# Routing two chunks in the expert phase, choosing part 1 inside the last chain, and a PSUM bank for each of the last local tiles

## What is computed

```
a = x + global_latent_attn(rmsnorm(x, norm1_w))      # causal, 16 heads of 8, 4 key/value heads
a = a + local_gqa_attn(rmsnorm(a, norm2_w))          # causal, window of 32 keys
x = layernorm(x + a)
probs = sigmoid(x @ router_w.T + routing_bias)       # 8 experts
topk_p, topk_idx = top_k(probs, 2); topk_p /= sum(topk_p)
shared = (silu(x @ sg_w.T) * (x @ su_w.T)) @ sd_w.T
routed = sum over the 2 experts of topk_p * (silu(x @ wg[e].T) * (x @ wu[e].T)) @ wd[e].T
out = layernorm(x + shared + routed)
```

## Time and profile before

| what | us |
|---|---|
| median of 3 runs | 815.64 |
| lowest and highest | 811.75, 817.01 |
| the profiled execution | 819.62 |
| its span, first to last instruction | 817.9 |
| TensorE busy / VectorE busy | 641.7 / 518.1 |
| ScalarE busy / GpSimd busy | 406.9 / 376.5 |

### The profile page before, as it was taken

One profiled execution on the slowest core, in us unless ns is written; L12 is line 12 of the kernel. 1 busy time (PEld: TensorE's weight loads), 2 busy tenths in 40 slices (PEclk: granted clock), 3 DMA queues, 4 the chain that ended last, 5 costly groups with the idle time before them and its releaser, 6 DMA issues. The chain is left out here.

```text
span 817.9 us, 12163 instructions
## 1 busy us (share of the span) xinstructions
PE 641.7 (78%) x3942; PEld 350.3 (43%) x3942; DVE 518.1 (63%) x1340; ACT 406.9 (50%) x562; POOL 376.5 (46%) x414
## 2 busy tenths in 40 slices
PE   2337888988998887899976697975278999996991
PEld 1203332233453333444333243444266676664881
DVE  2566864456996557898459966475854774332685
ACT  0225766866766775567754454740012544343244
POOL 3397633424544443443322676702324147777511
PEclk9958888999999998999878797996568999999895
DMA  8133555400000000000000001100003123323332
GB/s 253 55 107 104 188 160 186 146 1 1 1 1 1 1 1 14 2 13 14 14 1 0 25 27 37 34 14 0 7 21 93 41 71 91 105 82 114 115 104 65
DMA packets 38126, 47.22 MB, mean 58 GB/s; under 512 B 8961, under 2 KB 35233, under 8 KB 37409
## 3 DMA queue, kind: packets, MB, share of 16 engines
q1 hardware_dynamic: 26976, 35.10, 14.2%
q0 software_dynamic: 4352, 9.05, 3.2%
q10 hardware_dynamic: 6736, 2.30, 1.2%
HBM read 35.29 MB, written 28.98 MB: 79 GB/s over the span
## 5 line engine op out<-in xcount | busy, mean ns | idle before, releaser
L781 ACT ACTIVATE prob<-ps_s 128x1024 f32<-128x1024 f32 x320 | 309.4, 1025 | 197.9 <-PE ps_s L1109 129.0
L1142 PE MATMUL ps_v<-prob,va 128*32 128x512 f32 x1152 | 173.1, 685 | 16.5 <-POOL prob L703 15.8
L1109 PE MATMUL ps_s<-qs,ks 32*128 32x512 f16 x576 | 106.5, 410 | 33.9 <-ACT prob L781 30.5
L916 DVE STREAM_TRANSPOSE sums<-ps_v 128x512 f32<-128x512 f32 x64 | 45.7, 714 | 86.3 <-PE ps_v L1136 44.1
L703 POOL TENSOR_SCALAR_AFFINE_SELECT prob<-prob 128x1024 f32<-128x1024 f32 x64 | 70.4, 1118 | 51.1 <-ACT prob L781 50.7
L1109 PEld LDWEIGHTS ps_s<-qs,ks 32*128 32x128 f16 x576 | 25.2, 92 | 146.7 <-ACT prob L781 97.5
L1349 POOL DMA_INDIRECT y_rows<-y,to_row x72 | 69.5, 966 | 37.0 <-issue 19.8
L1136 PE MATMUL ps_v<-prob,vd 128*128 128x256 f32 (+1 forms) x312 | 72.1, 384 | 17.3 <-DVE marked L936 17.2
L1371 ACT ACTIVATE gated<-ps_gu 128x512 f32<-128x512 f32 x52 | 31.0, 598 | 89.1 <-PE ps_gu L1565 67.4
L1136 PEld LDWEIGHTS ps_v<-prob,vd 128*128 128x128 f32 x312 | 59.3, 215 | 31.4 <-DVE prob L943 15.7
L1565 PE MATMUL ps_gu<-weights,rows_t 128*128 x144 | 68.0, 594 | 0.5 <-ACT rows_t L1376 0.5
(11 more groups left out here) (200 smaller groups left out, 1036.9 us busy)
## 6 DMA issues: line engine op xcount, KB each, us to landing
x_rows<-in_blank SPq DMA_DIRECT2D x8, 2112.0 KB, 9.4
rows<-x_rows SPq DMA_DIRECT2D x72, 66.0 KB, 2.1
chosen_y<-y_rows SPq DMA_DIRECT2D x8, 512.0 KB, 6.8
weights<-in_weights SPq DMA_DIRECT2D x1, 3456.0 KB, 13.6
marked<-in_hidden SPq DMA_DIRECT2D x4, 512.0 KB, 5.1
out<-result ACTq DMA_DIRECT2D x8, 256.0 KB, 2.3
r_in<-in_hidden SPq DMA_DIRECT2D x7, 256.0 KB, 2.8
y_rows<-y,to_row POOLq DMA_INDIRECT x72, 2.4
```

Of the source, the lines that this page charges most:

```text
L781: act.activation(probs_at(n, 0, SLOT_COLS), scores_at(n, 0, SLOT_COLS), ACT.Exp, scale=HD ** -0.5 / GAIN ** 2).then_inc(exped, 1)
L916: dve.transpose(sums[:].rearrange("p r b v -> p (r b v)"), ps_v[bank_of[q]][:].rearrange("p r q -> p (r q)")).then_inc(sums_turned, 1)
L1109: last = pe.matmul(scores_at(n, j * BANK, BANK).rearrange("p (r q) -> p r q", r=REP), ks[b % QUERY_BATCHES][rows, kt * P:(kt + 1) * P], qs ...
L1142: last = pe.matmul(bank[g * VW:(g + 1) * VW, :, :], va[b % VALUE_BATCHES][:, kt, g, :], probs_at(n + g // 2, g % 2 * BANK, BANK).rearrange ...
```

## The change

Chunks 6 and 7 are both routed in the expert phase (`LATE = CHUNKS - 2`), which adds, norms and turns eight tiles there: the statistics on VectorE in steps 1 and 2, the norm itself as eight Identity activations on ScalarE in step 3 (`late_tokens`), the turns at steps 4 and 5, logits of all eight tiles at step 6 and the exponential at step 7. The turn at step 45 goes. Chunk 6 has no chain in the attention phase any more. Part 1 is chosen at steps 326 to 345, and all its 16 scatters are issued at steps 352 to 367. Its blocks are laid in two lists (`LISTS`), rows of chunks 0 to 3 first, and `EARLY_PAIRS` falls to 24. The last part's 16 scatters stand ahead of pair 6. The `combine` of chunks 0 to 3 moves to steps 34, 36, 37 and 38, that of the others up by one. There are four `result` buffers. The last four local tiles have their slots at steps 356 to 359, the last two of them use the side banks `ps_p`, and the projection follows two steps behind the product.

The diff, cut to its core:

```diff
 TURNS = 3
 LOCAL_STEPS = 2
-POST = 3
+LAST_LOCALS = 4
+POST, LAST_POST = 3, 2
 VALUE_BATCHES, QUERY_BATCHES = 3, 3
 SHARES = 3
 FINAL = SHARES - 1
...
 SHARE_ENDS = tuple(2 * tiles - EXPERTS for tiles in TILES_SO_FAR[:-1]) + (POSITIONS,)
 SHARE_BEGINS = (0,) + SHARE_ENDS[:-1]
 SHARE_POSITIONS = tuple(end - begin for begin, end in zip(SHARE_BEGINS, SHARE_ENDS))
-EARLY_POSITIONS = SHARE_BEGINS[FINAL] + 2 * SHARE_TILES[0] + EXPERTS - 1 - SHARE_ENDS[0]
+EARLY_POSITIONS = SHARE_BEGINS[FINAL] + EXPERTS
 CAPACITY = TILES
 X_BLOCKS = EXPERTS * CAPACITY + EXPERTS
-LISTS = tuple(EXPERTS * (2 if part == FINAL else 1) for part in range(SHARES))
-LATE = CHUNKS - 1
-TO_ROW, FIRST_EXPERT, GAIN, WEIGHT = range(D, D + 4)
+LISTS = tuple(EXPERTS * (2 if part else 1) for part in range(SHARES))
+LATE = CHUNKS - 2
+TO_ROW, FIRST_EXPERT, GAIN_AT, WEIGHT = range(D, D + 4)
 ROW = D + 4
 SCAN, ENDS = 8, 8
 SHIFTS = tuple(tuple(2 ** n for n in range(6) if 2 ** n < tiles) for tiles in SHARE_TILES)
...
           (34, "choose", "experts")]
 SENDS_FROM = 29
 SEND = [(SENDS_FROM + i * 3 // 2, "send", i) for i in range(2 * SHARE_TILES[0])]
-SENT_INSIDE = 8
 INSIDE = [CHOOSE + SEND,
-          CHOOSE[:1] + [(34, "choose", "prob"), (34, "choose", "first"), (35, "choose", "second"), (35, "choose", "third"),
-                        (36, "choose", "weights"), (37, "choose_rank"), (38, "choose", "totals"), (38, "choose", "scan"),
-                        (39, "choose", "slots"), (40, "choose", "slot1"), (41, "choose", "slot2")]
-          + [(47 + i, "send", i) for i in range(SENT_INSIDE)]]
-ROUTE_AT = {0: 172, 1: 188, 2: 210, 3: 0, 4: 0, 5: 0, 6: 344}
+          CHOOSE[:1] + [(17, "choose", "prob"), (17, "choose", "first"), (20, "choose", "second"), (20, "choose", "third"),
+                        (26, "choose", "weights"), (28, "choose_rank"), (34, "choose", "totals"), (34, "choose", "scan"),
+                        (35, "choose", "slots"), (35, "choose", "slot1"), (36, "choose", "slot2")]
+          + [(43 + i, "send", i) for i in range(2 * SHARE_TILES[1])]]
+ROUTE_AT = {0: 172, 1: 188, 2: 210, 3: 0, 4: 0, 5: 0}
 P_DVE = [["one_plus", "prob", "top1", "is1", "place1", "first1", "mark", "pick1", "others",
...
-    for i, _ in enumerate(range(B * TPB - sum(len(v) for v in LOCAL_INSIDE.values()))):
-        add_local((j + 1 + i) % 2)
-        step += LOCAL_STEPS
+    left = B * TPB - sum(len(v) for v in LOCAL_INSIDE.values())
+    for i in range(left):
+        add_local(SIDES + i - (left - SIDES) if i >= left - SIDES else (j + 1 + i) % 2)
+        step += 1 if i >= left - LAST_LOCALS else LOCAL_STEPS
...
+        def sums_bank(q):
+
+            return ps_v[bank_of[q]][:] if bank_of[q] < 2 else ps_p[bank_of[q] - 2][:].rearrange("p (r q) -> p r q", r=REP)
+
...
                         pe.wait_ge(rope, rope_value(chunk_number[chunk], 1, "values"))
-                if w == firsts[q] and before[q] is not None:
+                if w == firsts[q] and bank_of[q] >= 2:
+                    take_side(bank_of[q] - 2, added, q + 1)
+                elif w == firsts[q] and before[q] is not None:
                     pe.wait_ge(added, before[q] + 1)
...
 MARKED_AT = {ROUTED_AT[m] + 2: m // GROUP for m in range(0, PAIRS, GROUP)}
 LATE_BEGIN, LATE_AT = 1, 4
 PICK_AT = {1: {"blocks": 4, "ends": 4, "starts": 5, "past": 5, "rows": 6, "experts": 6},
-           2: {"prob": 7, "first": 7, "second": 8, "third": 8, "weights": 8, "totals": 10, "scan": 10, "slots": 11, "slot1": 11,
+           2: {"prob": 8, "first": 8, "second": 9, "third": 9, "weights": 9, "totals": 11, "scan": 11, "slots": 11, "slot1": 12,
                "slot2": 12, "blocks": 13, "ends": 13, "starts": 14, "past": 14, "rows": 15, "experts": 15}}
 TURN_AT = {c: SHARED_AT[c * CT // 2] - 3 if c * CT // 2 in SHARED_LAST else SHARED_FIRST.index(c * CT // 2) // 2 - 1
-           for c in range(LATE)} | {LATE: LATE_AT}
-GATHERED_AT = {0: 37, 1: 38, 2: 39, 3: 40, 6: 47, 4: 48, 7: 49, 5: 50}
+           for c in range(LATE)} | {c: LATE_AT + c - LATE for c in range(LATE, CHUNKS)}
+LOGITS_AT = LATE_AT + 2
+GATHERED_AT = {0: 34, 1: 36, 2: 37, 3: 38, 6: 46, 4: 47, 7: 48, 5: 49}
 LAST = 2
 IN_TIME = [f for f, when in GATHERED_AT.items() if when <= SHARED_AT[2 * f] + LAST]
 END_AT = {f: SHARED_AT[2 * f + 1] + LAST if f in IN_TIME else when + 1 for f, when in GATHERED_AT.items()}
 END_STEPS = 2
 FINALS_AFTER = PAIRS - 1
-BEFORE_SEND = {2: 2}
+FINAL_SENDS = 6
+RESULTS = 4
...
         def _(pool):
             def late_power():
 
                 pool.wait_ge(l_dve, nth(LATE_STEPS, "var_eps"))
-                pool.tensor_tensor(rstd[CHUNKS][:], rstd[CHUNKS][:], st["half"][:], ALU.pow).then_inc(l_rstd, 1)
-
-            def dispatch(part):
-
-                if part == FINAL:
-                    pool.wait_ge(p_dve[part], picked(part, "index2"))
-                    pool.wait_ge(l_dve, nth(LATE_STEPS, f"token{CT - 1}"))
-                for i in range(SENT_INSIDE if part < FINAL else 0, 2 * SHARE_TILES[part]):
-                    t, k = SHARE_FIRST[part] + i // 2, i % 2
-                    pool.indirect_dma_start(
-                        x_rows, bass.IndirectOffsetOnAxis(ap=index[:, t, k:k + 1], axis=0), st["marked"][:, t, :], None
-                    ).then_inc(dispatched[part], 16)
+                pool.tensor_tensor(l_rstd[:], l_rstd[:], st["half"][:], ALU.pow).then_inc(l_powered, 1)
+
+            def dispatch():
+
+                pool.wait_ge(p_dve[FINAL], picked(FINAL, "index2"))
+                pool.wait_ge(l_tokens, LATE_TILES)
+                for t in range(SHARE_FIRST[FINAL], TILES):
+                    for k in range(2):
+                        pool.indirect_dma_start(
+                            x_rows, bass.IndirectOffsetOnAxis(ap=index[:, t, k:k + 1], axis=0), st["marked"][:, t, :], None
+                        ).then_inc(dispatched[FINAL], 16)
 
             def send_y(m):
 
@@ -1352,13 +1363,12 @@
 
             def power(f):
                 pool.wait_ge(f_dve[f], nth(END, "var_eps"))
-                pool.tensor_tensor(rstd[f][:], rstd[f][:], st["half"][:], ALU.pow).then_inc(f_rstd, 1)
-
-            dispatch(1)
+                pool.tensor_tensor(rstd[f][:], rstd[f][:], st["half"][:, 0:CT], ALU.pow).then_inc(f_rstd, 1)
+
             late_power()
             for m in range(PAIRS):
-                if m in BEFORE_SEND:
-                    dispatch(BEFORE_SEND[m])
+                if m == FINAL_SENDS:
+                    dispatch()
                 send_y(m)
...
-                act.dma_start(out.rearrange("b (t p) d -> p (b t) d", p=P)[:, chunk(f), :], result[f % 2][:]
-                              ).then_inc(out_stored[f % 2], 16)
+                place = results.index(f)
+                act.wait_ge(f_result, CT * (place + 1))
+                act.dma_start(out.rearrange("b (t p) d -> p (b t) d", p=P)[:, chunk(f), :], result[place % RESULTS][:]
+                              ).then_inc(out_stored[place % RESULTS], 16)
 
...
+            def late_tokens():
+
+                act.wait_ge(l_dve, nth(LATE_STEPS, "shift"))
+                for t in range(LATE_TILES):
+                    of = x[:, LATE * CT + t, :]
+                    act.activation(of, of, ACT.Identity, bias=l_shift[:, t:t + 1], scale=l_rstd[:, t:t + 1]).then_inc(l_tokens, 1)
 
             for c in turned_at(-1):
                 move_tokens(c)
@@ -1405,9 +1424,11 @@
                         move_rows(SEQUENCE[step + 1][1])
                 if 0 <= step - 1 < len(SEQUENCE) and routed(step - 1):
                     move_hidden(step - 1)
+                if step == LATE_AT - 1:
+                    late_tokens()
                 for c in turned_at(step):
                     move_tokens(c)
-                if step == LATE_AT + 2:
+                if step == LOGITS_AT + 1:
                     act.wait_ge(l_dve, nth(LATE_STEPS, "logit"))
                     act.activation(choice["logits"][FINAL][:], choice["logits"][FINAL][:], ACT.Exp, scale=-1.0).then_inc(p_exped[FINAL], 1)
...
+                if n == LATE_BEGIN + 1:
+                    for t in range(LATE_TILES):
+                        late_step()(f"moments{t}", dve.bn_aggr, l_moments[:, t, :], l_stats[:, t, :])
+                    late_step()("var_eps", dve.tensor_scalar, l_rstd[:], l_moments[:, :, 1], LN_EPS, None, ALU.add)
                 if n == LATE_AT - 1:
-                    dve.wait_ge(l_rstd, 1)
-                    scale(late_step(), "token", x[:, late, :], x[:, late, :], CHUNKS)
-                if n == LATE_AT + 1:
+                    dve.wait_ge(l_powered, 1)
+                    late_step()("shift", dve.scalar_tensor_tensor, l_shift[:], l_moments[:, :, 0], -1.0, l_rstd[:], ALU.mult, ALU.mult)
+                if n == LOGITS_AT:
                     dve.wait_ge(l_logits, 1)
-                    late_step()("logit", dve.tensor_tensor, choice["logits"][FINAL][:, SHARE_TILES[FINAL] - CT:, :],
```

(3 more changed lines are left out.)

102 lines of the change are left out of this document (48 added, 54 removed).

## The result

The changed kernel takes 806.64 us (median of 19 runs, 804.25 to 817.09) against 817.01 us (19 runs, 811.75 to 823.46) for the kernel before, measured beside it: ratio 0.988, 95% interval 0.986 to 0.991. It is faster by some 10 us (1.2 per cent, with 1 outside the interval), half of the 20 forecast, and just above the predicted range.

What follows compares the result with a forecast made beforehand. Routed steps run through TensorE almost alone, with time lost at four places; -11.2 + 6.5 - 10.9 - 4.4 = -20.0 us takes the median from 815.64 to 795.6 us, range 787 to 806.

Steps and rivals of the forecast that it cites:

- Last chain: End of attention phase: `k_rows` at 580.7 instead of 585.98, first scores of the last tiles at 584.0 instead of 591.41.
- Last four tiles: Last local tiles of attention: TensorE ends at 601.7, but GpSimd's 16 scatters close the phase at 604.1; -11.2 us with the chain.
- so E moves to 604.4: Expert phase start, 615.54 before: 16 scatters cost 20.2 us from 583.9, end at 604.1 and set the start; -11.2 us.
- E: The start of the expert phase, set 0.27 us behind the last work before it; 615.54 before, 604.4 forecast.
- a start 0.27 us behind the last work before it: End of attention phase: margin assumed between the last work there and the expert phase's start.
- attention gives half: Rival, chance 0.13: pushed chain or slower scatters beside VectorE's copies leave -5.2 instead of -11.2 us in the attention phase; 801.6 us.
- First expert steps: First twelve steps of the expert phase: they lose 6.5 us against before, bounds 4.5 and 9.5.
- The wait for `chosen_y`: Routed steps, first `combine` at step 34: VectorE waits only 0.6 us for gathered data; -10.9 us, bounds -11.5 and -4.0.
- End: Program's end: turn at step 45 and the store's wait go; -4.4 us, bounds -5.6 and -2.4.
- the last `normed` could start: Program's end: without the 2.41 us store wait, the last `normed` starts at 809.93 + 0.12 instead of 813.32, 3.2 us.
- the two middle rivals: The gather still waits, chance 0.14, 804.4 us; the attention phase gives half its gain, chance 0.13, 801.6 us.

Runs made afterwards that it cites:

- the run with the choice behind: Changed kernel with eight of part 1's 16 scatters in the attention phase and part 1's choice behind the last chain's split: ratio 0.983 to the kernel before, repeated 0.985.
- eight scatters inside: Changed kernel with eight of part 1's 16 scatters in the attention phase, eight at the expert phase's head: ratio 0.971 to the kernel before, 799.87 us; repeated 0.984.

## Why the prediction was half right

**Last chain: right in sum (-6.7, forecast -7.4), with its causes unweighed.** `k_rows` came at 585.39, 581.5 on the clock of before (forecast 580.7); `xt` was pushed 0.8 us as said. I took the weight operations for nothing; they and the picks push the split by 1.6 us (0.85 forecast), measured against the run with the choice behind. I named the choice and chunk 6's norm together. The run with the choice behind shows that the norm's leaving brought 4.5 and the choice's place 2.2.

**Last four tiles: the step "so E moves to 604.4" failed.** The tiles took 15.1 us (17.7 forecast), and that GpSimd, not TensorE, closes the phase was right. From the landmark, E was 6.7 us later than forecast. 0.7 came with the chain. 2.0 came from the scatters: they ended 22.1 us behind the first score, and 16 of them took 21.95 us, not 20.2, because I had taken a row from a stretch where VectorE is busy 37 per cent of the time and never with a 128x1024 product. Beside such products of the band (L949, VectorE busy 8.4 of 10.8 us) three of the first six took 1.33, 1.96 and 1.52 us, where 0.96 is usual. The remaining 4.0 is "a start 0.27 us behind the last work before it": I measured that margin where VectorE was last, and used it where GpSimd was: there the start comes 4.24 us behind the last scatter, 4.00 of them GpSimd's drain. The rival "attention gives half" had nearly the right size (-5.2, measured -4.5) and named slower scatters, yet put the mechanism in the chain and the copies. With eight scatters inside, the two segments together are 15.0 us shorter than before (55.17 less 40.21), more than the 11.2 forecast for all sixteen.

**First expert steps: right (+6.6, forecast +6.5)**, with some luck, by errors that cancel: the idle stretch was 3.78 us (3.6 forecast), the half clock cost 1.7 and not 0.8, other steps less. The Trainium skill, "TensorE: Matmul & The Clock Gate" (HAM oscillation), was weighed there; the traces agree with it for 3.8 us idle (0.56 behind the stop), and show no fall of the clock behind 1.1 (late tokens on VectorE). The Trainium skill's rule in "ScalarE: Activation LUTs" (Rules for kernel authors) gives additions and multiplications to VectorE; following it was worth 4.4 us of the 6.6. Its reason is VectorE's speed per element, the gain here came from ScalarE's queue.

**The wait for `chosen_y`: right (-10.7, forecast -10.9).** It waited 0.1 us where I had 0.6; with 28 pairs the whole wait came back, and TensorE's stop of 8.3 us cost 11.4, 3.1 beyond its length (3.4 in the prediction).

**End: the term "the last `normed` could start" 3.2 us earlier held, its use did not.** The last shift's distance to the last store shrank as said, and 1.0 of the 1.2 us before it came. But of the 3.2 us only 0.7 reached the end, since GpSimd's drain closed the program 2.9 us behind the store. -1.7 instead of -4.4.

So 20.0 - 10.3 = 9.7 us were missed: 6.7 at the first block's end, 2.7 at the second's, 0.3 elsewhere. Both drains had rows in the trace of before, ending 3.3 us and 7.9 us behind GpSimd's last work. The prediction rests on timelines and tables of stretches, which have no such rows. The range ended at 806 and the time came to 806.6, because I took the two middle rivals one at a time and no term's bounds held a cost common to both ends.

## What to carry to other kernels

Before moving work to the end of a block, list the block's end rows by line and ask of each engine when it would leave its drain, not when its last instruction ends; GpSimd's comes 3 to 8 us after its last work, so give it the earliest finish. Where several engines end at one place, an edit on one that isn't the last is worth nothing by itself (four banks: 0 us alone, 4.9 once GpSimd was out of the way), so test such edits in pairs. And compare traces by segments from a common landmark: the same instructions ended up to 12 us apart.
